# Global attention and feed-forward in one block, with double-buffered loads and a new queue order

## The reference

```python
K = 2.0 * jnp.einsum('chn,hnl->chl', Ct, V).real            # tokenizer, V = exp(log(dA) * l)
...
ga = _masked_softmax(jnp.einsum('bhqd,bhkd->bhqk', q, gk) * scale, g_mask)
out_global = jnp.einsum('bhqk,bhkd->bhqd', ga, gv)
out = (1.0 - gate) * out_local + gate * out_global
out = out.transpose(0, 2, 1, 3).reshape(B, L, D)
return out @ w_out + b_out
...
return jnp.einsum('bsh,oh->bso', _q_act(x), _q_w(w))        # each feed-forward product
```

## Time and profile before

| | us |
|---|---|
| median of three runs | 1720.04 (1719.72 to 1722.29) |
| the profiled execution | 1721.08 |
| its span | 1719.3 |
| tokenizer, up to its barrier | about 0 to 225 |
| landmark attention | about 890 to 981 |
| global attention | about 1089 to 1364 |
| feed-forward | about 1365 to 1719 |

### The profile page before, as it was taken

One profiled execution on the slowest core, in us unless ns is written; L12 is line 12 of the kernel. 1 busy time (PEld: TensorE's weight loads), 2 busy tenths in 40 slices (PEclk: granted clock), 3 DMA queues, 4 the chain that ended last, 5 costly groups with the idle time before them and its releaser, 6 DMA issues. The chain is left out here.

```text
span 1719.3 us, 30582 instructions
## 1 busy us (share of the span) xinstructions
PE 1479.1 (86%) x11218; PEld 977.6 (57%) x11218; DVE 1283.0 (75%) x2388; ACT 1002.9 (58%) x2539; POOL 578.3 (34%) x600
## 2 busy tenths in 40 slices
PE   2177759999999999999978888598888499999997
PEld 2177736766776667766765666465555144444443
DVE  8999937777777777777725265278888399999996
ACT  7799827777877887787733142277675223333332
POOL 0000014445544545445500000046666433333333
PEclk9555569999999999999977799799999799999999
DMA  2022252332323332332262063446665235444443
GB/s 80 1 59 52 62 155 81 100 121 98 91 91 112 101 103 91 103 125 91 73 219 80 13 220 112 130 134 186 185 185 157 71 83 107 99 99 99 104 99 86
DMA packets 233093, 182.98 MB, mean 106 GB/s; under 512 B 163568, under 2 KB 165104, under 8 KB 232944
## 3 DMA queue, kind: packets, MB, share of 16 engines
q1 hardware_dynamic: 232944, 181.03, 36.5%
HBM read 93.95 MB, written 59.77 MB: 89 GB/s over the span
## 5 line engine op out<-in xcount | busy, mean ns | idle before, releaser
L1056 PE MATMUL al_ps<-w,al_xT 128*128 128x512 f32 (+2 forms) x1024 | 350.6, 496 | 0.0
L1056 PEld LDWEIGHTS al_ps<-w,al_xT 128*128 128x128 f32 x1024 | 191.7, 192 | 126.9 <-issue 107.3
L2206 POOL TENSOR_TENSOR ff_zq<-ff_z,ff_back 128x1024 bf16<-128x1024 fp8e4 x64 | 122.4, 1912 | 227.0 <-DVE ff_z L2229 227.0
L449 PE MATMUL tk_ps<-tk_w,tk_l 128*128 128x64 f32 x512 | 113.0, 422 | 79.0 <-DVE tk_w L418 51.9
L449 PEld LDWEIGHTS tk_ps<-tk_w,tk_l 128*128 128x128 f32 x512 | 110.4, 332 | 81.6 <-issue 81.6
L2173 ACT ACTIVATE ff_sg<-ff_gate 128x1024 f32<-128x1024 f32 x64 | 65.6, 1025 | 148.7 <-PE ff_gate L2252 148.7
L751 POOL TENSOR_TENSOR al_qv<-al_qv,al_qe 128x512 f32<-128x512 f32 x48 | 63.2, 1316 | 233.4 <-PE al_ps L1115 233.4
L2271 PE MATMUL ff_acc<-wdT,ff_zT 128*128 128x512 bf16 x512 | 122.9, 383 | 6.7 <-DMA ff_zT<-ff_zq 6.7
L2252 PE MATMUL ff_up<-wuT,xqT 128*128 128x512 bf16 x512 | 122.2, 382 | 3.0 <-DVE ff_z L2221 3.0
L2252 PE MATMUL ff_gate<-wgT,xqT 128*128 128x512 bf16 x512 | 122.7, 383 | 0.9 <-ACT ff_sg L2173 0.9
L2031 PE MATMUL ag_ps<-ag_w,ag_aT 128*128 128x512 f32 x256 | 114.3, 600 | 1.7 <-ACT ag_ps L1865 1.7
(11 more groups left out here) (294 smaller groups left out, 3292.7 us busy)
## 6 DMA issues: line engine op xcount, KB each, us to landing
al_hx<-h_s SPq DMA_DIRECT2D x36, 256.0 KB, 2.7
o_s<-al_o SPq DMA_DIRECT2D x32, 272.0 KB, 2.2
h_s<-tk_w SPq DMA_DIRECT2D x16, 512.0 KB, 3.8
v_s<-al_v SPq DMA_DIRECT2D x32, 256.0 KB, 2.2
k_s<-al_kT SPq DMA_DIRECT2D x32, 256.0 KB, 2.4
q_s<-al_qT SPq DMA_DIRECT2D x32, 256.0 KB, 2.6
lt_k<-k_s SPq DMA_DIRECT2D x16, 512.0 KB, 5.0
lt_v<-v_s SPq DMA_DIRECT2D x16, 512.0 KB, 3.7
```

The lines of the kernel that those rows point to most:

```text
L449: ins = pe.matmul(o, L[:, u, 0, t], R[:, u, t], start=True, stop=True)
L1056: ins = pe.matmul(out, xT[:, T, k], w[:, k, cols], start=False, stop=True, skip_group_check=True)
L2206: pool.tensor_tensor(zq[:, u].rearrange("p (k s) -> p k s", s=QB), z8[:, u].rearrange("p (k s) -> p k s", s=QB), back[:, u, :, None].to_br ...
```

## The change

1. Tokenizer: VectorE sums only CS = 13 of 16 tokens; for the other three TensorE multiplies both parts, one after the other, into the same PSUM.
2. Landmark attention: a 512-column bf16 product into a bank already read (stream) behind each of the first three g of every L1343 group, 12 in all. Its result is not used.
3. Global attention: gvr, gate, o and h get two buffers, their loads a semaphore per buffer and waits one element looser; SP has a new order. The wait for b_rows moves to the first bias, the first keys ahead of the wait for TensorE's dummy products. On GpSimd quantized stands behind the gated sum and ahead of scaled, one element later (j-2).
4. Global attention and feed-forward share one block, one PSUM tensor of 8 banks and no barrier between them. The loops of the attention end one turn earlier; what is left of element 15 (normalised rows, maxima, exponents, scaling, clip, quantized rows, transposes) is called as tail between the first units of the feed-forward. The first gate product of each element waits for its transposes. y of the feed-forward lies in bias_rows; lmfT, l2qT and roT are freed with the landmark stages.

```diff
+    CS = 13
...
-                dve.tensor_tensor(L[:, u, 0], L[:, u, 0], L[:, u, 1], ALU.add).then_inc(l_ready, 1)
+                dve.tensor_tensor(L[:, u, 0, 0:CS], L[:, u, 0, 0:CS], L[:, u, 1, 0:CS], ALU.add).then_inc(l_ready, 1)
...
-                    ins = pe.matmul(o, L[:, u, 0, t], R[:, u, t], start=True, stop=True)
+                    ins = pe.matmul(o, L[:, u, 0, t], R[:, u, t], start=True, stop=t < CS)
+                    if t >= CS:
+                        ins = pe.matmul(o, L[:, u, 1, t], R[:, u, t], start=False, stop=True)
...
+            def stream(bank):
+                pe.matmul(ps[:, bank], K.identb[:], K.wdT[:, 0], start=True, stop=True)
...
+                    if g < 3:
+                        stream(4 * u + 1 + g)
...
-    gvr = sb("gvr", [P, D])
+    gvr = sb("gvr", [P, 2, D])
...
-    qT, gate, o, h = sb("qT", [P, 2, 2, KC, P]), sb("gate", [P, 2, H]), sb("o", [P, 2, D]), sb("h", [P, 2, D])
+    qT, gate, o, h = sb("qT", [P, 2, 2, KC, P]), sb("gate", [P, 2, 2, H]), sb("o", [P, 2, 2, D]), sb("h", [P, 2, 2, D])
...
         def residual(i):
-            if i:
-                sp.wait_ge(h1_t, 2 * i)
-            sp.dma_start(h[:], h_s[:, i].rearrange("(b p) d -> p b d", p=P)).then_inc(h_in, 16)
+            if i >= 2:
+                sp.wait_ge(h1_t, 2 * i - 2)
+            sp.dma_start(h[:, i % 2], h_s[:, i].rearrange("(b p) d -> p b d", p=P)).then_inc(h_in[i % 2], 16)
...
+        values(1)
         residual(0)
+        gates(1)
+        local(1)
+        residual(1)
         for j in range(-3, BATCH):
-            if 0 < j + 3 < BATCH:
-                gates(j + 3)
-            if 0 < j + 2 < BATCH:
-                local(j + 2)
+            if 2 <= j + 3 < BATCH:
+                local(j + 3)
+            if some(j - 2):
+                quantized(j - 2)
+            if 2 <= j + 4 < BATCH:
+                gates(j + 4)
             if some(j):
                 store(j)
-            if 0 < j + 1 < BATCH:
-                residual(j + 1)
-            if some(j - 1):
-                quantized(j - 1)
-            if some(j + 5):
+            if 2 <= j + 2 < BATCH:
+                residual(j + 2)
+            if 2 <= j + 5 < BATCH:
                 queries(j + 5)
-            if some(j + 4):
-                values(j + 4)
-        quantized(BATCH - 1)
-        sp.wait_ge(h1_out, 16 * BATCH)
-        sp.wait_ge(xt_in, 32 * BATCH)
+            if 2 <= j + 5 < BATCH:
+                values(j + 5)
+        quantized(BATCH - 2)
...
     def gpsimd(pool):
-        for j in range(-1, BATCH + 1):
+        for j in range(-1, BATCH):
             if some(j + 1):
                 gated_sum(j + 1)
+            if some(j - 2):
+                quantized(j - 2)
             if some(j - 1):
                 scaled(j - 1)
             if some(j):
                 deviations(j)
-            if some(j - 1):
-                quantized(j - 1)
+        quantized(BATCH - 2)
...
         def bias(i, T):
+            if i == T == 0:
+                act.wait_ge(s_b, 16)
...
+        keys(0)
         act.wait_ge(s_bits, 1)
         masked(0)
-        keys(0)
         values(0)
-        act.wait_ge(s_b, 16)
...
-            if some(j):
+            if some(j) and j + 1 < BATCH:
                 normalised(j)
...
+    gate, up = ps[:, 0:2], ps[:, 4:6]
+    acc = [ps[:, bank] for bank in (3, 7)]
...
         def residual(t, T):
             sp.wait_ge(res_r.sem, res_r.done(t, 2))
+            sp.wait_ge(attended.h1_out, 16 * (t // 2 + 1))
...
             turn(i, 1)
+            if i == 0:
+                tail(1)
...
                 silu(i, j)
+                if i == j == 0:
+                    tail(0)
...
+                if i == 0 and j < 2:
+                    tail(j)
...
     def tensor(pe):
+        pe.wait_ge(attended.sub_r, BATCH)
...
             pe.wait_ge(sg_r.sem, sg_r.done(q, 1))
+            if q % NU == 0:
+                pe.wait_ge(attended.xt_in, 32 * (q // NU + 1))
...
+        @block.sync
+        def _(sp):
+            quantized = attended.sync(sp)
+            sync(sp, lambda j: quantized(last))
+        @block.gpsimd
+        def _(pool):
+            scaled, quantized = attended.gpsimd(pool)
+            gpsimd(pool, lambda j: (scaled, quantized)[j](last))
+        @block.scalar
+        def _(act):
+            normalised = attended.scalar(act)
+            scalar(act, lambda j: normalised(last))
+        @block.vector
+        def _(dve):
+            block_maxima, exponents, quantized = attended.vector(dve)
+            def tail(j):
+                if j == 0:
+                    block_maxima(last)
+                    exponents(last)
+                else:
+                    quantized(last)
+            vector(dve, tail)
+        @block.tensor
+        def _(pe):
+            attended.tensor(pe)
+            tensor(pe)
...
-                attention_global(nc, A, K, h_s, q_s, o_s, gv_s, h1_s)
-            with phase(nc):
-                ffn(nc, K, h1_s, out)
+                attention_and_ffn(nc, A, K, h_s, q_s, o_s, gv_s, h1_s, out)
```

1042 lines of the change are left out of this document (522 added, 520 removed).

## The result

The changed kernel takes 1706.5 us (median of 4 runs, 1704.8 to 1707.4); the kernel before, in the same set of runs, 1719.9 (1717.6 to 1722.3). The ratio is 0.9916, 95% interval 0.9895 to 0.9936, so 0.84% faster; the two medians stand 13.4 us apart. The profiled execution took 1707.05 us with a span of 1705.2; before it was 1721.08 and 1719.3, so the traces differ by 14.1. The forecast was 1701.0, 5.5 too low, with the time inside its range of 1692 to 1710.

What follows compares the result with a forecast made beforehand. Barrier-divided stages each had their own bound (VectorE in the feed-forward, TensorE in the landmarks). Tokenizer -1.5, landmarks -3.0, start -3.8, turns -3.8, junction -6.9 gave -19.0: 1721.08 to 1702.1, median 1701.0, range 1692 to 1710.

Steps and rivals of the forecast that it cites:

- its ring: Tokenizer loop: fractions, sine, phases and rounding close over the shorter add, so a chunk falls from 9.00 only to 8.84 us.
- Landmark streams: Landmark stage: twelve extra products cost 2.9 to 5.7 us but partly hold TensorE's clock; -3 us, ends -8 and +5.
- rival (b): Landmark stage: the extra products are paid and buy nothing, +3.7 us, total 1707.7; chance 0.18.
- Start: Start of global attention: with the b_rows wait moved to the first bias, the first exp starts earlier; -3.8 us.
- The keys' step: Start of global attention: keys ahead of the dummy products gain 0, since the first scores start when q lands.
- Steady turns: Global attention turns: double-buffered h removes six waits on the residual's load; -3.8 us, ends 0 and -4.5.
- right behind the second residual, 3 us earlier: Steady turns, SyncE's queue: the h1 store goes out behind two transposes but ahead of the eight value loads.
- rival (d): Steady turns: the store or the memory's load came last, so the 3.8 us stay, total 1704.8; chance 0.12.
- GpSimd's order: Steady turns: the gated sum no longer stands behind the quantized rows; effect 0, with 1.3 us of cover for VectorE's L1982.
- Junction: Attention to feed-forward: the h1 loads behind element 14's transposes come last; L2221 9.5 us earlier, net -6.9 us.
- the term of 2.6 us: Feed-forward: element 15's maxima (1.22), four exponent steps (0.75) and clip (0.61) add 2.6 us of VectorE work.
- Rival (e): Global attention turns: GpSimd's new order becomes the bound; beyond 1.3 us of stretch each turn pays, 1739 at 4 us; chance 0.03.

## Why the prediction was right, and where it wasn't

The forecast of -19.0 became -14.1 between the two traces. The differences by row of the table are +2.2 (start), +1.7 (landmarks), -0.7, -0.7, -0.1, +0.8 (turns), -0.5 (junction), +1.8 (feed-forward) and +0.4, in all +4.9. Part of the nearness is luck: 1.4 us of the gain lie in two stretches for which nothing was forecast (0.7 of it is the keys, the rest scatter) and 1.1 in an interval that TensorE's clock shortened, while the same clock hid the tokenizer's 1.5.

- **Tokenizer: right** in its ring (8.82 against 8.84 us) and its size (-1.6 at the stage's end over fourteen profiles, -1.5 forecast). In the table's first row it is hidden by scatter of TensorE's clock behind the stage. What the prediction lacked is this scatter: its range had bounds for each edit and none for stretches that don't change. The same instructions took 78.1 to 84.1 us from first still to first lk.
- **Landmark streams: the size is not borne out, and not excluded.** -3 was taken as half of a reckoned 6.5; ten profiles against four give +0.1, within about 3 us, between the forecast and rival (b). The price was mis-sized: 2.9 to 5.7 us were reckoned from the mask rows, and groups at one clock show 1.5 to 2.9. The reason given for -3, that a group had run at the high clock right behind 512-column products, does not carry it: here the clock fell between two such products. The Trainium skill (TensorE: Matmul & The Clock Gate, What's actually happening) says that sustained activity releases the clock. The fall at 922 us does not speak against that, since TensorE had stood idle twice shortly before, for 1.76 and 1.29 us; it shows only that three such products in a group did not hold the clock.
- **Start: right**, -3.9 against -3.8, and shown alone in the kernel before. **The keys' step failed**: 0 was forecast, 0.6 to 0.7 measured. It read the wait of the weight load, which ended with q. The product itself had waited 3.29 us for ScalarE's keys; with the keys first, it starts when q has landed.
- **Steady turns: right that the six load waits go, wrong on what follows.** The step that failed is that the store goes out "right behind the second residual, 3 us earlier". Before, it left 3.1 us behind the last h1 add (1222.24+0.68 to 1226.03) and 6.5 ahead of the next; after, it leaves 6.1 behind and 3.7 ahead. The prediction took the queue to be free when the store's turn comes; in fact it stands at the value loads of the turn before, which are asked for before their buffer is free, and then the value loads (4.5 us), the local output's load and two transposes (2.5) go first. So rival (d) came true in part: waits of 0.8 to 3.8 us on the store in eight profiles took the place of 3.8 on the load, and of the -3.0 in the table 1.1 is the clock's. Keeping the old queue order, with each load one turn later, or doubling h1 takes the waits away entirely; both were run. **GpSimd's order** was costed at 0, with a rival that it could hurt; undoing it costs 9.6 us. The step failed because it asked only which engine waits for GpSimd, not what GpSimd's quantized rows wait for: the transposes of the element before, which the change had moved. Whether the order gains anything by itself is not run (the kernel before with this order alone). In the changed kernel it is what makes the new queue order bearable.
- **Junction: right**, 10.0 against 9.5, and by the mechanism named: the h1 loads are last, behind element 14's transposes. The runs that move the loads or the silu show it from two sides.
- **Feed-forward: the term of 2.6 us was mis-sized**; it measured 4.4. Order of time after, VectorE and GpSimd in the first units:
```profile
1359.33 1.91 POOL L2212 TENSOR_TENSOR ff_zq<-ff_z,ff_back 128x1024 bf16<-128x1024 fp8e4 x1 [14.84 <-DVE ff_z L2236]
...
1360.29 0.99 DVE L1981 TENSOR_SCALAR ag_eb<-ag_eb 128x32 uint32<-128x32 uint32 x1
...
1369.34 1.91 POOL L1797 TENSOR_TENSOR ag_xq<-ag_x,ag_back 128x1024 bf16<-128x1024 fp8e4 x1
...
1370.03 1.25 DVE L1628 TENSOR_SCALAR ff_eb<-ff_eb 128x32 uint32<-128x32 uint32 x1
```
  Two exponent steps that take 0.18 alone took 0.99 and 1.25, and end at 1361.28 and 1371.28, each 0.03 to 0.04 behind GpSimd's multiply (1361.24, 1371.25): 0.81+1.07 = 1.9 us more. With the 2.6 that makes 4.5, and it is all in the first three intervals, 7.89, 5.82 and 6.29 us in place of 5.22 each. The step that failed is "four exponent steps (0.18 each, 0.75)", priced as if they ran alone. The prediction had seen the same pattern on L1931, and in the kernel before that step takes 1.24 us in the 13 turns in which a GpSimd multiply runs beside it and 0.23 in the other three. It cited the exclusive lock of the port pair (the Trainium skill, SBUF - State Buffer, SBUF: two separate sides), for VectorE with two SBUF inputs. The two stretched steps have one input, so the rule as quoted does not cover them; the same section names a second case, a two-port mode of VectorE, and the trace does not show the mode. That GpSimd's multiply holds them up is argued from the common end times; no run here shows that the lock is the cause.
- The forecast itself, that no mechanism turns the sign, held. Rival (e), slower by GpSimd's new order, did not come: the order's danger lies on the other side. Its place (VectorE's inv behind the quantized rows) did show up, 1.90 us, in the run with single buffers.

## What to carry to other kernels

When a step moves within an engine's queue, list both who waits for it and what it waits for, down to the transfer that still reads its buffer. Parts that cost nothing or lose when undone alone may be a set: here single buffers with the queue's old order cost 10.6 us in the attention, and GpSimd's old order alone 9.6. A load that is asked for before its buffer is free stops the whole queue behind it: in the run that asks one turn later, among other moves, no such wait is left. Behind a removed wait, compute how far the next one is away (issue to use, against the landing time): a store that lands in 3.5 us, issued 3.5 us before VectorE is ready for its next add, is just not hidden. Work moved into a stage of a busy engine costs its time beside the other engines of that stage, not its time alone. And at a new junction, look for the queue item that waits in front of the one that is needed; moving one item ahead gave 9.3 us, twice the 4.7 net of the overlap itself. Before a difference in a stretch is put down to the change, compare the granted clock over it: 1.1 us of the attention's gain here was the clock's.

## What the runs showed of the hardware

- Stretches of unchanged code scatter by several us between executions, and TensorE's clock goes with them: the first block product came 1.8 us apart in two profiles of the same instructions. First still to first lk took 78.1 to 80.0 us in the seven profiles in which TensorE stood at 1.2 GHz for 3.4 to 6.8 us of it, and 80.2 to 84.1 in the seven with 10.2 to 20.5. In the longest, the run with two blocks, the granted clock was 0.66 from 1025 to 1040 us; in one of the shortest, 78.5 us with the h1 loads first, it was 1.00 there.
- The clock fell between two 512-column products inside a group in which TensorE was busy (921.03 took 0.38 us, 922.05 took 0.59), behind idle stretches of 1.76 and 1.29 us. Three such products in a group of 17-column products cost 0.38 us together at the high clock (3.75 to 4.13) and 0.72 at the low one (7.01 to 7.73).
- Beside a GpSimd multiply of 1.91 us a VectorE step on 128x32 elements took 0.99 or 1.25 us instead of 0.18, and one on 128x64 took 1.24 instead of 0.23, each ending 0.03 to 0.08 behind the multiply. The reciprocal just ahead of the latter (L1927) ran beside such a multiply in 13 turns and took 0.55 us with it or without.
- The median time from the issue to the landing of the h1 store, 512 KB, was 5.1 us in the kernel before, 3.5 in the changed one and 3.2 in the one with the old queue order. Within the kernel before, the last three stores, which no loads precede in the queue, landed in 2.8 to 3.1 us and the others in 5.0 to 5.6. That what is queued ahead of it makes the difference is read from these orders, not tested alone.
